# Context in 128-row tiles and squared lengths as three bf16 parts, in a gated cross-attention and feed-forward kernel

## The reference, cut to what matters

```python
def _pairwise_euclidean(a, b):
    aa = jnp.sum(a * a, axis=-1)[:, None]
    bb = jnp.sum(b * b, axis=-1)[None, :]
    ab = a @ b.T
    return jnp.sqrt(jnp.maximum(aa + bb - 2.0 * ab, 0.0))
...
D = _pairwise_euclidean(small, large)
R = _dtw_cost(D)
i_idx, j_idx, valid = _backtrack(R, T_small, T_large)
...
x = x + jnp.tanh(g_xattn[0]) * _L0_xattn_ref(ctx_1024, _layernorm(x, axis=-1))
```

## Time and profile before

| | |
|---|---|
| median of three runs | 648.78 us (646.63 to 649.3) |
| the profiled execution's own time | 643.75 us |
| its span, first to last instruction | 641.9 us |
| its mean granted TensorE clock | 0.795 of full |
| TensorE busy | 420.9 us, 66% of the span |
| VectorE busy | 433.1 us, 67% |
| ScalarE busy | 264.8 us, 41% |
| GpSimd busy | 110.0 us, 17% |
| first load to the start of the shear (L1693) | 0.80 to 42.0 us |

### The profile page before, as it was taken

One profiled execution on the slowest core, in us unless ns is written; L12 is line 12 of the kernel. 1 busy time (PEld: TensorE's weight loads), 2 busy tenths in 40 slices (PEclk: granted clock), 3 DMA queues, 4 the chain that ended last, 5 costly groups with the idle time before them and its releaser, 6 DMA issues.

```text
span 641.9 us, 10182 instructions
## 1 busy us (share of the span) xinstructions
PE 420.9 (66%) x3448; PEld 301.2 (47%) x3448; DVE 433.1 (67%) x1714; ACT 264.8 (41%) x627; POOL 110.0 (17%) x209
## 2 busy tenths in 40 slices
PE   2998799623393303557888888899999655406306
PEld 2667685511273103444666665677555553106303
DVE  4645999899746796958886775775454575473573
ACT  4744544812303541015454553665543452351340
POOL 7900000000042891525810000000000000000000
PEclk9997699655585755569898998999999887855556
DMA  4560004292007992001699895700200271000002
GB/s 134 155 159 1 2 2 155 72 200 76 2 1 113 135 137 19 1 0 36 182 114 182 127 215 52 74 1 2 104 28 1 79 256 59 2 0 1 1 1 58
DMA packets 45769, 47.16 MB, mean 73 GB/s; under 512 B 5197, under 2 KB 43926, under 8 KB 44694
## 3 DMA queue, kind: packets, MB, share of 16 engines
q1 hardware_dynamic: 45718, 46.51, 35.3%
HBM read 37.80 MB, written 8.60 MB: 72 GB/s over the span
## 4 chain that ended last, share of the span: by engine, by line
PE 52%; DVE 25%; ACT 9%; issue 6%; SPq 3%; POOL 3%; DMA 2%; DVEq 0%; ACTq 0%
PE ps L1958 7%; PE ps L1912 4%; DVE PR L982 4%; ACT below L1593 4%; PE ps L1899 4%; PE ps L1734 3%; PE ps L1888 3%; PE ps L1742 3%; SPq L548 3%; PE ps L1798 3%; PE ps L1874 2%; PE ps L2084 2%; DMA ctxP<-in_ctx 2%; POOL ct L744 2%; DVE prod L978 2%
## 5 line engine op out<-in xcount | busy, mean ns | idle before, releaser
L1143 DVE TENSOR_REDUCE negm<-ps 112x1 f32<-112x375 f32 x128 | 65.8, 543 | 18.8 <-PE ps L1888 15.7
L1564 ACT ACTIVATE E<-ps 125x448 f32<-125x448 f32 x96 | 52.0, 544 | 59.4 <-PE ps L1899 59.3
L1888 PE MATMUL ps<-ks,qs 96*112 96x375 bf16 x128 | 44.0, 353 | 14.6 <-issue 10.6
L2057 PE MATMUL ps<-cnt,same 128*128 128x3 bf16 (+4 forms) x40 | 6.8, 170 | 61.8 <-ACT below L1593 43.4
L1912 PE MATMUL ps<-E,v 125*32 125x112 f32 x768 | 42.8, 274 | 0.0
L1899 PE MATMUL ps<-qs,ks 99*125 99x112 bf16 x384 | 40.1, 228 | 1.6 <-DVE qs L1164 1.0
L1131 DVE TENSOR_REDUCE acts<-gel 128x4 f32<-128x448 f32 x32 | 19.8, 620 | 29.3 <-ACT gel L1527 29.3
L1899 PEld LDWEIGHTS ps<-qs,ks 99*125 99x125 bf16 x384 | 34.5, 140 | 10.4 <-issue 6.3
L727 POOL CAST kp<-kx 128x750 bf16<-128x750 f32 x8 | 6.5, 811 | 167.5 <-ACT path L1479 142.1
L2057 PEld LDWEIGHTS ps<-cnt,same 128*128 128x128 bf16 (+1 forms) x40 | 4.3, 109 | 65.0 <-issue 65.0
L1527 ACT ACTIVATE gel<-ps 128x448 f32<-128x448 f32 x32 | 17.3, 544 | 29.3 <-PE ps L1958 29.3
(11 more groups left out here) (363 smaller groups left out, 1133.4 us busy)
## 6 DMA issues: line engine op xcount, KB each, us to landing
ks<-key_parts SPq DMA_DIRECT2D x48, 187.5 KB, 8.5
piw<-fn_process_input_weights SPq DMA_DIRECT2D x8, 1024.0 KB, 4.9
key_parts<-kp SPq DMA_DIRECT2D x16, 281.2 KB, 4.7
ctx_again<-in_ctx SPq DMA_DIRECT2D x7, 512.0 KB
ctxP<-in_ctx SPq DMA_DIRECT2D x8, 375.0 KB
keys<-kx SPq DMA_DIRECT2D x16, 187.5 KB, 2.1
kx<-keys SPq DMA_DIRECT2D x8, 375.0 KB, 6.7
patn<-in_L_ffn_input_patterns SPq DMA_DIRECT2D x1, 2048.0 KB, 17.9
```

The costliest lines, as they stand in the source:

```text
L1143: drain(dve.tensor_reduce(negm[:, n:n + 1], bank(nm)[0:S, 0:SC], AX.X, ALU.max, negate=True), nm)
L1564: drain(fn(E[:, (KCH * f + c) % 6, :], bank(nm)[0:KC, 0:4 * S], ACT.Exp), nm)
L1888: fill(mm(bank(nm)[0:S, 0:SC], qs[0:SR, u // 4 % 3, n, :], ks[0:SR, u // 4 % 3, n, :], start=True, stop=True), nm)
```

## The change

The context of a batch is loaded by two transfers instead of one: rows 0 to 255 as two tiles of 128 partitions, and rows 247 to 374 as a third tile of 128 partitions, so that nine rows stand in two tiles. The transposes write 128 columns each; the third overwrites nine columns with the same values. `aa` has 128 rows. GpSimd splits it, batch by batch, into three bf16 parts whose sum is the float32 value (`split_squares`, four operations, each waiting for the one before), in an order that goes ahead of `pick`, `UU` and `v1` and takes the zeroing of `meet` with it. TensorE transposes the 9 columns of parts as bf16, and the products that add them are three bf16 products with 9 rows against a new 9 x 3 selection tile `of_tile`, which GpSimd makes among the constants. `zerob` shrinks to two columns and is read by broadcast. Beside the hunks below, a semaphore `aa_split` is added to the list of names.

```diff
@@ -20,6 +20,8 @@
 HID, HT = 1024, 8
 NH, HD = 16, 16
 KC, KCH = 125, 3
+ROW0 = (0, 128, SC - 128)
+COLS = ((0, 128), (128, 256), (256, SC))
 
 
 K_PARTS = (0, 1, 0, 1, 0, 2)
@@ -259,7 +261,7 @@
         sd = ra.take("sd", [S, B])
         rstd = ra.take("rstd", [S, B])
         bb = ra.take("bb", [S, B])
-        aa = ra.take("aa", [KC, B, KCH])
+        aa = ra.take("aa", [128, B, KCH])
         bqT = ra.take("bqT", [128, 2])
         bkT = ra.take("bkT", [128, 2])
         bqs = ra.take("bqs", [128, 2])
@@ -306,7 +308,7 @@
         c0 = max(rk.at, rl.at)
         rc = Region(c0)
 
-        ctxP = rc.take("ctxP", [KC, KCH, B, D])
+        ctxP = rc.take("ctxP", [128, KCH, B, D])
         rz = Region(c0)
         LG = rz.take("LG", [128, T + 1, PW], BF16)
         PR = rz.take("PR", [128, T + 1, PW], BF16)
@@ -322,7 +324,7 @@
         r_at = rx.at
         rn0 = Region(r_at)
         ln0T = rn0.take("ln0T", [128, DH, TOK])
-        aaT = rn0.take("aaT", [KCH, B, KC])
+        aaT = rn0.take("aaT", [3 * KCH, B, 128], BF16)
         path = Region(r_at).take("path", [128, B, CT, S])
         R = rx.take("R", [128, T + 1, RB + 1])
         rd = Region(max(rx.at, rn0.at, r_at + 4 * B * CT * S))
@@ -330,7 +332,10 @@
         meet = [rd.take(f"meet{d}", [128, KB, 128]) for d in range(2)]
         scratch = Region(rw.at + 4 * CT * B * D)
         lanes_at = scratch.take("lanes_at", [128, 2, 2, 32], BF16)
-        zerob = scratch.take("zerob", [128, 512], BF16)
+        zerob = scratch.take("zerob", [128, 2], BF16)
+        aa_rest = scratch.take("aa_rest", [128, KCH])
+        aa_parts = scratch.take("aa_parts", [128, B, KCH, 3], BF16)
+        of_tile = scratch.take("of_tile", [3 * KCH, KCH], BF16)
         dmin = scratch.take("dmin", [128, RB])
         rmin = scratch.take("rmin", [128, 3 * RB])
         prod = scratch.take("prod", [128, 2 * RB], BF16)
@@ -545,7 +550,9 @@
         def _(sp):
             sp.dma_start(x[:, :, :], x_in.rearrange("b s d -> s b d")).then_inc(loaded["x"], 16)
             for b in range(B):
-                sp.dma_start(ctxP[:, :, b, :], ctx_in[b].rearrange("(c p) d -> p c d", p=KC)).then_inc(loaded[f"ctx{b}"], 16)
+                sp.dma_start(ctxP[:, 0:2, b, :], ctx_in[b, 0:256, :].rearrange("(c p) d -> p c d", p=128)
+                             ).then_inc(loaded[f"ctx{b}"], 16)
+                sp.dma_start(ctxP[:, 2, b, :], ctx_in[b, ROW0[2]:SC, :]).then_inc(loaded[f"ctx{b}"], 16)
             for i, w in enumerate((wq_in, wk_in, wv_in, wo_in)):
                 sp.dma_start(wnat[:, i, :, :], w.rearrange("(c p) d -> p c d", p=128)).then_inc(loaded["attnW"], 16)
             sp.dma_start(w1n[:, :].rearrange("p (c d) -> p c d", c=HT),
@@ -648,6 +655,7 @@
                 did(pool.memset(t[:, :], 0.0))
             for t in (ones, same[0], same[1], onesb):
                 did(pool.memset(t[:, :], 1.0))
+            did(pool.memset(of_tile[:, :], 1.0))
             did(pool.memset(eps[:, :], 1e-5))
             did(pool.memset(no_magic[:, :], -MAGIC))
             did(pool.memset(magic[:, :], MAGIC))
@@ -659,6 +667,11 @@
                 did(pool.affine_select(out=t[:, :], in_=t[:, :], compare_op=ALU.not_equal, fill=v, base=0,
                                        pattern=[[-1, 128]], channel_multiplier=1))
 
+            did(pool.affine_select(out=of_tile[:, :], in_=of_tile[:, :], compare_op=ALU.is_ge, fill=0.0, base=0,
+                                   pattern=[[-3, KCH]], channel_multiplier=1))
+            settle()
+            did(pool.affine_select(out=of_tile[:, :], in_=of_tile[:, :], compare_op=ALU.is_ge, fill=0.0, base=2,
+                                   pattern=[[3, KCH]], channel_multiplier=-1))
             did(pool.affine_select(out=skew[0][:, :], in_=skew[0][:, :], compare_op=ALU.not_equal, fill=1.0,
                                    base=KB - 1, pattern=[[-1, T + KB - 1]], channel_multiplier=1))
             did(pool.affine_select(out=skew[1][:, :], in_=skew[1][:, :], compare_op=ALU.not_equal, fill=1.0,
@@ -693,7 +706,26 @@
             settle()
             pool.memset(warm[:, :], 0.0).then_inc(consts_ready, 1)
 
+            def split_squares(b):
+
+                pool.wait_ge(aa_ready, b + 1)
+                did(pool.tensor_copy(aa_parts[:, b, :, 0], aa[:, b, :]))
+                settle()
+                did(pool.tensor_tensor(aa_rest[:, :], aa[:, b, :], aa_parts[:, b, :, 0], ALU.subtract))
+                settle()
+                did(pool.tensor_copy(aa_parts[:, b, :, 1], aa_rest[:, :]))
+                settle()
+                pool.tensor_tensor(aa_parts[:, b, :, 2], aa_rest[:, :], aa_parts[:, b, :, 1], ALU.subtract
+                                   ).then_inc(aa_split, 1)
+                pool.wait_ge(aa_split, b + 1)
+
             pool.wait_ge(ln_ready, B)
+            split_squares(0)
+            for d in range(2):
+                did(pool.memset(meet[d][:, :, :], 0.0))
+                split_squares(d + 1)
+            for b in range(3, B):
+                split_squares(b)
             for j, part in enumerate(Q_PARTS):
                 did(pool.tensor_copy(pick[:, part, :, HD * j:HD * j + HD],
                                      identb[:, :].rearrange("p (e d) -> p e d", d=HD)))
@@ -701,9 +733,6 @@
 
             pool.memset(hand(UU[:, 0, 1:2], [[PW, T], [2, RB]]), 1.0).then_inc(uu_ready, 1)
             pool.memset(v1[:, :, :, :], 1.0).then_inc(ones_v_ready, 1)
-            for d in range(2):
-                did(pool.memset(meet[d][:, :, :], 0.0))
-            settle()
             for d in range(2):
                 for k in range(KB):
                     for at in (64 * d + k, 64 - 64 * d + KB - 1 - k):
@@ -1377,10 +1406,10 @@
             root(0)
             def squares(b):
 
-                act.wait_ge(loaded[f"ctx{b}"], 16)
+                act.wait_ge(loaded[f"ctx{b}"], 32)
                 for c in range(KCH):
                     settle()
-                    ins = fn(actscr[0:KC, 0:D], ctxP[:, c, b, :], ACT.Square, accum_out=aa[:, b, c:c + 1])
+                    ins = fn(actscr[:, 0:D], ctxP[:, c, b, :], ACT.Square, accum_out=aa[:, b, c:c + 1])
                     if c < KCH - 1:
                         did(ins)
                 ins.then_inc(aa_ready, 1)
@@ -1388,7 +1417,7 @@
             def square_rows(b):
                 nm = ("aaT", b)
                 wait_filled(act, nm)
-                drain(fn(aaT[:, b, :], bank(nm)[0:KCH, 0:KC], ACT.Copy), nm)
+                drain(fn(aaT[:, b, :], bankb(nm)[0:3 * KCH, 0:128], ACT.Copy), nm)
 
             squares(0)
             act.wait_ge(aa_ready, 1)
@@ -1651,19 +1680,20 @@
                     mm(bank(nm)[0:S, 0:SC], ln0T[:, h, S * b:S * b + S], ctxT[:, h, b, :], start=(h == 0), stop=False)
                 wait_drained(pe, ("aaT", b))
                 for c in range(KCH):
-                    ins = mm(bank(nm)[0:S, KC * c:KC * c + KC], ident[0:KCH, c:c + 1].broadcast_to([KCH, S]),
-                             aaT[:, b, :], start=False, stop=(c == KCH - 1))
+                    lo, hi = COLS[c]
+                    ins = mm(bank(nm)[0:S, lo:hi], of_tile[:, c:c + 1].broadcast_to([3 * KCH, S]),
+                             aaT[:, b, lo - ROW0[c]:hi - ROW0[c]], start=False, stop=(c == KCH - 1))
                 fill(ins, nm)
 
             def context_transposes(b):
 
-                pe.wait_ge(loaded[f"ctx{b}"], 16)
+                pe.wait_ge(loaded[f"ctx{b}"], 32)
                 for h in range(DH):
                     nm = ("ctxT", b, h)
                     claim(pe, nm)
                     for c in range(KCH):
-                        ins = tr(bank(nm)[:, KC * c:KC * c + KC], ctxP[:, c, b, 128 * h:128 * h + 128],
-                                 ident[0:KC, 0:KC])
+                        ins = tr(bank(nm)[:, ROW0[c]:ROW0[c] + 128], ctxP[:, c, b, 128 * h:128 * h + 128],
+                                 ident[:, :])
                     fill(ins, nm)
 
             context_transposes(0)
@@ -1672,8 +1702,8 @@
             for b in range(B):
                 nm = ("aaT", b)
                 claim(pe, nm)
-                pe.wait_ge(aa_ready, b + 1)
-                fill(tr(bank(nm)[0:KCH, 0:KC], aa[:, b, :], ident[0:KC, 0:KC]), nm)
+                pe.wait_ge(aa_split, b + 1)
+                fill(tr(bankb(nm)[0:3 * KCH, 0:128], aa_parts[:, b, :, :].rearrange("p c e -> p (c e)"), identb[:, :]), nm)
                 if b + 2 < B:
                     context_transposes(b + 2)
                 if b == 0:
@@ -1775,7 +1805,7 @@
             for j in range(7, -1, -1):
                 nm = ("path", j)
                 claim(pe, nm)
-                mm(bank(nm)[:, :], identb[:, :], zerob[:, :], start=True, stop=True)
+                mm(bank(nm)[:, :], identb[:, :], zerob[:, 0:1].broadcast_to([128, 512]), start=True, stop=True)
                 taus = range(min(8 * j + 7, T - 1), 8 * j - 1, -1)
                 for tau in taus:
```

(4 more changed lines are left out.)

## The result

The changed kernel takes 652.13 us (median of 20 runs, 646.74 to 663.48) against 646.9 us for the kernel before on the same chip (20 runs, 639.86 to 653.74). The ratio is 1.0072, interval 1.0047 to 1.0097: slower by 0.5 to 1.0%, some 4.7 us, where 642.2 us and a gain of 6.6 had been forecast. The profiled execution of the changed kernel takes 652.11 us, its span is 650.4. (The profiled execution of before lies 3.2 us under its own median here, so the two profiles lie further apart than the medians.)

What follows compares the result with a forecast made beforehand. TensorE was taken to bound the distance loop, whose lead carries to the shear and everything behind. -1.7, -3.75 and -1.15 us give -6.6, so 648.78 - 6.6 = 642.2 us; range 637.5 to 646.1.

Steps and rivals of the forecast that it cites:

- Loads: Context loads on 128 partitions: assumed 290 GB/s against 120, 1.3 us a batch against 3.2; both TensorE waits on context go.
- Constants: GpSimd's constants: smaller zero fill, one fill and two selects added; between -0.5 and +0.7 us, taken as +0.2.
- S: Time from the end of a batch's squares to its split on GpSimd: 0.8 to 2.1 us, taken as 1.3.
- Adding products: TensorE's distance loop: three bf16 passes replace six float32 ones; 0.25 us taken, saving 0.57 a batch.
- Batch: One batch of TensorE's distance loop: 2.35 us instead of 2.92, about ScalarE's own 2.38.
- First part: Up to TensorE's take of aa of batch 1, ending at 21.94 us before: -1.7 us.
- middle: Distance loop from 21.94 to 37.45 us before, 15.5 us; five batches of 2.35 make 11.75: -3.75 us.
- tail: Last two batches, 37.45 to 42.01 us before, 4.56 us; 1.7 each without context transposes, 3.4 together: -1.15 us.
- GpSimd's remaining work: GpSimd's work behind the last split: at most 20 us, ends by 54, with UU well ahead of 54.6, when wanted.
- The stages behind the shear keep their lengths, so the gain arrives whole: Everything after the shear: no change in length, so the 6.6 us gained by the shear's start reaches the total.
- The rivals: GpSimd becomes the bound (6 in 100), loads stay narrow (6 in 100), TensorE's clock falls in the tail (4 in 100).
- The last test that the prediction names: If the shear starts early but the meeting rows do not, the stages behind do not carry the gain.

Runs made afterwards that it cites:

- e3: The changed kernel with 24 more clearing products of 128 columns in the path stage, so TensorE's later instructions stand where they stood before: 646.90 us, 1.0004 of before.

## Why the prediction was wrong, step by step

- **Loads.** Right; they came at 350 GB/s, the assumption was 290, and the waits on context are gone.
- **Constants.** 0.2 us late had been taken; GpSimd's last one starts at 10.05 us in both kernels.
- **S.** 1.3 us had been taken; it is 1.06 (18.60 to 19.66). The nearest row was the copy, at 0.20, also for the two-input operations, and VectorE's copies did not hold them. Aa of batch 1 is taken at 19.80, forecast 20.2.
- **Adding products.** 0.30 us, forecast 0.25.
- **Batch.** 2.52 us, forecast 2.35: 0.05 of it in the adding products, 0.04 ahead of the context's transposes (0.15 for 0.11) and 0.07 in them (0.71 for 0.64), which the prediction had set to nothing.
- **The sum to the shear.** First part -2.14 (-1.7 forecast), middle -2.94 (-3.75: five batches in 12.57 us, 19.80 to 32.37), tail -0.78 (-1.15: 3.78 us to 36.15, since its two batches took 1.89 each and not 1.7). Together -5.86, forecast -6.6. The kernels without a stall carry 5.2 to 7.0 us to the meeting rows, so this part of the forecast stands.
- **GpSimd's remaining work: the step that failed.** The prediction asked when `UU` and `v1` are wanted, found 54.6 us and later, and costed their move behind the splits at nothing. They were in time. What it did not ask is what the fills would run beside at their new place: an operation of VectorE from SBUF to SBUF, with the shear's copies queued behind it and TensorE behind these. One operation of seven elements then took 7.04 us, and the whole gain of 5.9 us was gone at the meeting rows. The idea was at hand in the prediction itself, which weighed contention of GpSimd with VectorE for the four small operations of the split alone, and not for the two longest that GpSimd has.
- **"The stages behind the shear keep their lengths, so the gain arrives whole": failed as well.** The later stages grew by 4.6 us (2.5 to 4.6 over the six kernels at that place) without any of their own instructions changed, by the shift of TensorE's code. No row of before could have priced it; that 48 instructions were removed ahead of a stage with stops named "issue" could have been seen.
- **The rivals.** None of the three took place. The range was too narrow at its upper end since both failures lay in the stages that it took as fixed. (Its lower end adds up to 4.55 us and not 4.7, which changes nothing.) The last test that the prediction names (shear early, meeting rows not) is the one that came out.

The sum: a gain of 5.86 us to the shear's start, 5.93 given back by the meeting rows, 4.6 lost later, which is the measured 4.7 us. The 4.6 is what is left over, so that it closes proves nothing; what bears it out is that e3 gives 4.4 us of it back (1.0072 to 1.0004).

## What to carry to other kernels

When a long GpSimd operation is moved, list what VectorE does in its new stretch, not only when its result is due: a fill beside copies out of PSUM cost nothing here, beside a small operation from SBUF to SBUF it can hold the whole chain. Put such fills into stretches of the first kind, or cut them into pieces with a wait between. And when a change adds or removes instructions on TensorE, and a stage that it doesn't touch moves by some us, pad the program by a few small products, at more than one length, before looking for a cause in the data.

## What the runs showed of the hardware that was not expected

- **A fill holds VectorE by form, not by size.** Seven float32 elements a partition from SBUF took 7.04 us beside two fills in a row and 0.24 us beside none. An operation of one element a partition that was issued ahead of it (0.20, at 37.40, inside the fill of `UU`) and copies out of PSUM (0.54) were not held. GpSimd's copies of 8 elements, some 0.13 us apart, did not hold it for long (0.24). The Trainium skill (SBUF — State Buffer, Who interferes with whom) says that a VectorE operation in a two-port mode and a GpSimd operation lock each other out of a shared pair of ports for a whole instruction; and (VectorE: DVE Perf Modes, Mode 2×_2P) that such a mode halves one input along a dimension longer than one, and only where it lies in SBUF, not in PSUM. The rows with fills agree; those with the short copies do not decide. What the rows add is that the waiting operation did not come in between two fills that follow each other at once (held to 44.56), but did at a wait between them (38.82).
- **The place of code costs time.** 48 instructions less ahead of them, or 208 more, made the later stages 2.5 to 4.6 us longer; 256 more than a bad place left it bad. The block of 256 in the Trainium skill (the section cited above) agrees with these runs, but a period of 128, 64 or 32 would fit the places tried as well. If it is the crossing that costs, it is not hidden in this stage; no run shows that it is.
- **Three partitions.** The context's loads moved at 120 GB/s on 125 partitions and at 350 on 128, with the DMA engines' share going from 0.34 to 1.10. A batch also came in two transfers instead of one, and no run takes the two apart; but the weights, with one transfer for each matrix on 128 partitions, moved at 290 in the kernel before.
